# A graph layer and a mixture of experts on one core: the products' first two units taken by half and by quarters of Y, with the last rows and x blocks among them

## What is computed

```python
def gnn(H, W, A):                       # H = layernorm(x): (8, 2048, 128)
    HW = einsum('bnf,fo->bno', H, W)
    A_norm = relu((A + A.T) * 0.5)      # A = adj: (2048, 2048)
    D = sum(A_norm, axis=1)
    d_inv_sqrt = where(D > 0, D ** -0.5, 0)
    L_norm = eye(N) - d_inv_sqrt[:, None] * A_norm * d_inv_sqrt[None, :]
    return relu(einsum('nm,bmo->bno', L_norm, HW))

x = x + gnn(layernorm(x), W, adj)
tokens = layernorm(x)
# top 2 of 8 experts by softmax(tokens @ router_w.T), weights normalised to sum 1
# moe = tokens + sum over experts e of c_e * (gelu(tokens @ w1[e] + b1[e]) @ w2[e] + b2[e])
out = x + moe
```

## Time and profile before

| what | us |
|---|---|
| median of three runs (lowest, highest) | 878.23 (877.77, 879.5) |
| the profiled execution, own time | 877.46 |
| its span, first to last instruction | 875.7 |
| TensorE busy | 839.2 (96%) |
| VectorE busy | 639.1 (73%) |
| ScalarE busy | 476.0 (54%) |
| GpSimd busy | 324.7 (37%) |

### The profile page before, as it was taken

How to read it: one execution, slowest core, us unless ns; L and a number is a source line. 1 busy time by engine, 2 the same in 40 slices (tenths; PEclk the granted TensorE clock), 3 DMA queues, 4 the chain that set the end, 5 groups by cost and what they waited for, 6 DMA issues and landing times.

```text
span 875.7 us, 14324 instructions
## 1 busy us (share of the span) xinstructions
PE 839.2 (96%) x4098; PEld 697.3 (80%) x4098; DVE 639.1 (73%) x1553; ACT 476.0 (54%) x871; POOL 324.7 (37%) x318
## 2 busy tenths in 40 slices
PE   3687999999999999999999999999999999999998
PEld 3676788888888888888888777788888888888886
DVE  3678645479889644443515599999999999999997
ACT  2686523224333201021110488888888888888886
POOL 1893163474757545555445539101000000000000
PEclk9999999999999999999999999999999999999999
DMA  9991576686866257977778876778767777778772
GB/s 277 325 311 53 220 284 253 240 277 237 272 221 202 85 181 285 334 273 263 255 280 315 303 249 230 267 281 294 289 272 265 257 274 277 273 290 292 286 266 82
DMA packets 93472, 223.00 MB, mean 255 GB/s; under 512 B 8904, under 2 KB 60128, under 8 KB 81520
## 3 DMA queue, kind: packets, MB, share of 16 engines
q1 hardware_dynamic: 88304, 213.23, 68.7%
q0 software_dynamic: 2608, 8.33, 2.4%
q10 hardware_dynamic: 2512, 0.86, 0.4%
HBM read 157.89 MB, written 64.49 MB: 254 GB/s over the span
## 4 chain that ended last, share of the span: by engine, by line
PE 90%; DVE 4%; ACT 2%; DMA 2%; issue 1%; DVEq 0%; ACTq 0%; SPq 0%
PE bank L989 13%; PE bank L991 13%; PE bank L990 13%; PE bank L1489 6%; PE bank L1473 6%; PE bank L1475 6%; PE bank L1486 6%; PE bank L1474 6%; PE bank L1487 6%; PE bank L344 3%; PE bank L936 2%; PE bank L1495 2%; PE bank L474 1%; PE bank L325 1%; DMA b_sb<-in_L_ffn_b 1%
## 5 line engine op out<-in xcount | busy, mean ns | idle before, releaser
L1531 ACT ACTIVATE act_h<-bank,b_sb 128x512 f32<-128x512 f32 x256 | 176.3, 689 | 46.8 <-PE bank L1475 42.5
L1573 DVE TENSOR_TENSOR gated<-c_all,act_h 128x512 f32<-128x512 f32 x256 | 177.4, 693 | 25.5 <-ACT act_h L1531 20.4
L1578 DVE TENSOR_TENSOR g_lo<-gated,g_hi 128x512 fp32r<-128x512 f32 x256 | 175.1, 684 | 0.2
L1538 ACT ACTIVATE g_hi<-gated 128x512 fp32r<-128x512 f32 x256 | 159.5, 623 | 6.1 <-DVE gated L1573 6.1
L1449 POOL DMA_DIRECT2D out<-fin x31 | 23.6, 762 | 308.6 <-DVE fin L1586 308.6
L1105 POOL TENSOR_SCALAR z<-x,mv,rstd 128x128 f32<-128x128 f32 x128 | 106.9, 848 | 3.4
L989 PE MATMUL bank<-y_hi,stage 128*128 128x512 f32 x256 | 105.4, 412 | 2.8 <-issue 1.6
L1051 ACT ACTIVATE z_hl<-bank 128x512 fp32r<-128x512 f32 x32 | 19.1, 597 | 156.4 <-PE bank L936 156.4
L1473 PE MATMUL bank<-z_e,w_hi 128*128 128x512 f32 x256 | 102.8, 402 | 0.1
L1489 PE MATMUL bank<-g_lo,w_hi 128*128 128x512 f32 x256 | 100.9, 394 | 1.1 <-DVE g_lo L1578 1.1
L989 PE MATMUL bank<-y,stage 128*128 128x512 f32 x256 | 101.2, 395 | 0.0
(11 more groups left out here) (133 smaller groups left out, 1487.4 us busy)
## 6 DMA issues: line engine op xcount, KB each, us to landing
c_all<-c_scratch SPq DMA_DIRECT2D x64, 1024.0 KB, 8.1
s_scratch<-stage SPq DMA_DIRECT2D x14, 2048.0 KB, 8.2
stage<-s_scratch SPq DMA_DIRECT2D x14, 2048.0 KB, 8.0
z_e<-z_scratch SPq DMA_DIRECT2D x32, 512.0 KB, 7.3
z_scratch<-z_hl SPq DMA_DIRECT2D x31, 512.0 KB, 2.7
x_raw<-in_x SPq DMA_DIRECT2D x32, 256.0 KB, 6.7
x_res<-in_x SPq DMA_DIRECT2D x32, 256.0 KB, 7.0
r_e<-res_scratch SPq DMA_DIRECT2D x32, 256.0 KB, 2.7
```

Source lines behind the costliest of these rows:

```text
L1531: act.activation(v.act_h[e % R][:, :], ps_h[e % 2][:, :], ACT.Gelu, bias=v.b1_sb[:, e:e + 1]).then_inc(gelu_done, 1)
L1538: act.activation(v.g_hi[e % R][:, :], v.gated[e % R][:, :], ACT.Copy).then_inc(hi_done, 1)
L1573: dve.tensor_tensor(out=v.gated[e % R][:, :], in0=v.c_all[s][:, e, :], in1=v.act_h[e % R][:, :], op=ALU.mult).then_inc(gated_done, 1)
L1578: dve.tensor_tensor(out=v.g_lo[e % R][:, :], in0=v.gated[e % R][:, :], in1=v.g_hi[e % R][:, :].bitcast(FP32), op=ALU.subtract).then_inc(lo ...
```

## The change

Unit 0 and unit 1 are taken in six parts: blocks 15 to 8 of unit 0, then of unit 1; 7 to 4 of each; 3 to 0 of each. The adding loop over rows ends with row 11 (`ROWS_APART`); the last four rows, ten blocks, are transposed behind the first products. x blocks 12 to 15 are loaded behind all rows (14 and 15 into two new buffers in Y's own place), and turned and projected among products (`after_first`). GpSimd's column adds end with row 6 (`LAST` = 9); those of j = 8 and 7 go to VectorE too. Column sums stand in three clusters. Group 0 of unit 0's stage is turned behind row 8, group 1 behind row 9.

```diff
-    ps_x, ps_p = v.banks[4], [v.banks[5] if k % 2 or k >= v.MB else v.banks[3] for k in range(v.U)]
+    BANK = [3 if k in range(0, 12, 2) else 6 if k in (12, 14) else 5 for k in range(v.U)]
+    ps_x, ps_p = v.banks[4], [v.banks[b] for b in BANK]
...
-        free = k - 3 if k < MB else k - 1
+        if k in (14, 15):
+            sp.wait_ge(v.summed, v.until_tenth)
...
@@ -334,10 +347,8 @@
         pe.wait_ge(xt_copied, k + 1)
         if k == 0:
             pe.wait_ge(w_centred, 1)
-        elif k < MB:
-            wait(pe, hw_kept, k - 1)
-        elif k == MB:
-            pe.wait_ge(hw_kept, k)
+        elif k <= MB:
+            wait(pe, hw_kept, last_before(BANK, k))
...
-    FIRST = [(0, None), (0, 0), (0, 1), (1, None), (1, 0), (1, 1), (0, 2), (0, 3), (1, 2), (1, 3)]
+    FIRST = [(0, 0), (0, 1), (0, None), (1, None), (1, 0), (1, 1), (0, 2), (1, 2), (0, 3), (1, 3)]
...
-    LAST = 6
-    PARTS_AT = {14: ((0, 1),), 8: ((1, None), (1, 0), (1, 1)), 7: ((0, 2),), 5: ((0, 3),), 3: ((1, 2),), 1: ((1, 3),)}
-    RELU_AT = {13: 2, 12: 1, 11: 0}
-    ADD_AT = {13: 4, 11: 3, 10: 2, 9: 1}
-    JOBS = [2, 2, 2, 2, 1, 1, 1, 1, 1, 1, 1, 1, 0, 0, 0, 0]
+    LAST = 9
+    ROWS_APART = 12
+    JOBS = [2, 2, 2, 2, 1, 1, 1, 1, 0, 0, 0, 0, 0, 0, 0, 0]
+    EARLY = sum(JOBS)
...
+        for k in range(EARLY, MB):
+            pr.load(sp, k)
...
```

GpSimd, ScalarE, TensorE in `setup_stage`:

```diff
-            if r == 10:
+            if r == 9:
                 root(0)
+        pr.invert(pool, [EARLY])
         root(1)
+        for k in range(EARLY + 1, MB):
+            pr.invert(pool, [k])
...
+            for k in [k - 1 for k in jobs(r) if k]:
+                pr.keep(act, k)
+            if r == 8:
+                pr.keep(act, EARLY - 1)
+            if r in (8, 9):
+                st.high_group(act, 0, r - 8)
+            if r == 10:
+                st.high_direct(act, 0)
+                for m in range(15, 11, -1):
+                    y_high(m)
+        for m in range(11, 7, -1):
             y_high(m)
-            if m in RELU_AT:
-                relu(MB - 1 - RELU_AT[m], RELU_AT[m], 0)
-            if m == 7:
-                pr.keep(act, MB - 1)
-            for u, g in PARTS_AT.get(m, ()):
-                if g is None:
-                    st.high_direct(act, u)
-                else:
-                    st.high_group(act, u, g)
+        st.high_direct(act, 1)
+        st.high_group(act, 1, 0)
+        st.high_group(act, 1, 1)
+        for r in range(ROWS_APART, MB):
+            relu(r, MB - 1 - r, 0)
+        pr.copy_x(act, 12)
+        act.wait_ge(pr.xt_turned, EARLY)
+        act.wait_ge(pr.x_mv_done, EARLY)
+        st.high_group(act, 0, 2)
+        y_high(7)
+        y_high(6)
+        pr.keep(act, 12)
+        pr.copy_x(act, 13)
+        st.high_group(act, 1, 2)
+        y_high(5)
+        y_high(4)
+        pr.keep(act, 13)
+        pr.copy_x(act, 14)
+        st.high_group(act, 0, 3)
+        y_high(3)
+        pr.keep(act, 14)
+        pr.copy_x(act, 15)
+        st.high_group(act, 1, 3)
+        y_high(2)
+        pr.keep(act, 15)
+        y_high(1)
+        y_high(0)
...
         pe.wait_ge(small_in, 16 * v.small_loads)
         pr.average_w(pe)
-        for r, j in enumerate(ROWS):
+        for r, j in enumerate(ROWS[:ROWS_APART]):
...
+            if r == 6:
+                for k in (15, 14, 13, 12):
+                    column_sum(k)
+            if r == 8:
+                pr.project(pe, 11)
+                st.turn_group(pe, 0, 0)
+            if r == 9:
+                for k in (11, 10, 9, 8):
+                    column_sum(k)
+                pe.wait_ge(pr.hw_kept, EARLY - 1)
+                st.turn_group(pe, 0, 1)
+        v.column_sum, v.turn_last = column_sum, turn
```

VectorE in `setup_stage`, and TensorE in `graph_stage`:

```diff
+                st.low_group(dve, 0, 0)
+            if r == 10:
+                st.low_group(dve, 0, 1)
+                add_columns(8)
+                st.low_direct(dve, 0)
+                y_low(15)
+                y_low(14)
             if r == 11:
-                add_columns(5)
-        st.low_direct(dve, 0)
-        st.low_group(dve, 0, 0)
-        for m in range(MB - 1, -1, -1):
-            y_low(m)
-            if m in ADD_AT:
-                add_columns(ADD_AT[m])
-            for u, g in PARTS_AT.get(m, ()):
-                if g is None:
-                    st.low_direct(dve, u)
-                else:
-                    st.low_group(dve, u, g)
-                if (u, g) == (1, 0):
-                    degrees(1)
-            if m == 3:
-                outward()
+                add_columns(7)
+        y_low(13)
+        add(12, 3, 0)
+        y_low(12)
+        add(13, 2, 0)
+        y_low(11)
+        add(14, 1, 0)
+        y_low(10)
+        add(15, 0, 0)
+        y_low(9)
+        y_low(8)
+        st.low_direct(dve, 1)
+        st.low_group(dve, 1, 0)
+        st.low_group(dve, 1, 1)
+        for j in range(6, 0, -1):
+            add_columns(j)
+        pr.statistics(dve, 12)
+        degrees(1)
+        st.low_group(dve, 0, 2)
+        y_low(7)
+        y_low(6)
+        pr.statistics(dve, 13)
+        st.low_group(dve, 1, 2)
+        y_low(5)
+        y_low(4)
+        pr.statistics(dve, 14)
+        st.low_group(dve, 0, 3)
+        y_low(3)
+        pr.statistics(dve, 15)
+        st.low_group(dve, 1, 3)
+        y_low(2)
+        y_low(1)
+        outward()
+        y_low(0)
...
+            if u == 2 and i == 1:
+                st.turn_group(pe, 2, 2)
+                st.turn_group(pe, 2, 3)
+            if i == (5 if u == 2 else 2):
...
+        def after_first(u, m):
+            if u == 0 and m >= 8:
+                if m in (14, 13, 12, 11):
+                    v.turn_last(26 - m, m - 11, 0)
+                if m == 11:
+                    st.turn_group(pe, 1, 0)
+                if m == 10:
+                    st.turn_group(pe, 1, 1)
+            elif m >= 8:
+                if m == 14:
+                    pr.turn_x(pe, 12)
+                if m == 12:
+                    st.turn_group(pe, 0, 2)
+                if m == 11:
+                    pr.project(pe, 12)
+                    pr.turn_x(pe, 13)
+                if m == 10:
+                    for k in range(7, -1, -1):
+                        v.column_sum(k)
+                if m == 9:
+                    st.turn_group(pe, 1, 2)
+            elif u == 0:
+                if m == 6:
+                    pr.project(pe, 13)
+                    pr.turn_x(pe, 14)
+                if m == 4:
+                    st.turn_group(pe, 0, 3)
+                if m == 2:
+                    pr.project(pe, 15)
+            else:
+                if m == 6:
+                    pr.project(pe, 14)
+                    pr.turn_x(pe, 15)
+                if m == 5:
+                    st.turn_group(pe, 1, 3)
+                if m == 3:
+                    st.turn_group(pe, 2, 0)
+                    st.turn_group(pe, 2, 1)
-        for part in range(4):
+        for part, (a, b) in enumerate([(15, 8), (15, 8), (7, 4), (7, 4), (3, 0), (3, 0)]):
+            for m in range(a, b - 1, -1):
+                after_first(u, m)
```

57 lines of the change are left out of this document (16 added, 41 removed).

## The result

Seven runs of the changed kernel took 885.04 us in the median (883.15 to 888.16), seven of the kernel before beside them 878.23 (875.28 to 880.44). The ratio is 1.0086, 95% interval 1.0067 to 1.0105: slower by 5.9 to 9.2 us. The forecast was 884.3, range 880.8 to 887.5.

What follows compares the result with a forecast made beforehand. TensorE was taken to bound the kernel, with everything to win or lose before about 108 us. -8.5 + 7.0 + (8.3 - 1.3) + 0.6 = +6.1 us gave a forecast of 884.3 us, range 880.8 to 887.5.

Steps and rivals of the forecast that it cites:

- Step 1: From row 9's arrival to the first product: it starts at 70.1 instead of 78.6 us, 8.5 us earlier.
- Step 2: Behind the first product: four x blocks, ten blocks of rows 12 to 15 and eight column sums, 7.0 us.
- Step 3: New TensorE waits between the start and unit 2: 8.3 us against 1.3 before.
- Step 4: TensorE's lower clock over the first two blocks and row 12: 0.6 us later, bounds none and 1.6.
- a root doesn't hold VectorE up: Rival: at the start the diagonals run beside GpSimd's root; 2.3 us less, 882.0 us; chance 7%.
- the next rival: Rows 8 and 9 land earlier, first product at 65.6 us, deciding sign 66.1 or earlier; 879.2 us, not slower; chance 8%.
- y(7): After unit 1's upper half TensorE waits for the lower half's column sums, degrees, root, high and low part: 2.2 us.
- y(1): Behind x 15's projection TensorE waits, as ScalarE keeps that projection before making y(1)'s high part: 2.7 us.
- y(2): TensorE waits for unit 1's last transposes, copied by ScalarE, then the high and low part: 0.75 us.
- (a): At the start TensorE waits for y(13), behind VectorE's adds of row 11 and a column add: 1.8 us.
- (c): TensorE waits for y(5), behind VectorE's statistics of x 13, a low group and GpSimd's root: 0.85 us.
- more time at the low clock: Rival: the clock also falls behind the waits for y(7) and y(1), 0.7 and 1.6 us; 885.9 to 886.6 us; 25%.

Runs made afterwards that it cites:

- e3: Changed kernel plus 20 unread transposes of the identity ahead of the first product; 884.93 us, ratio 1.0079 to the kernel before.
- e8: Changed kernel plus unread transposes filling three waits: 20 at the start, 20 ahead of y(7), 24 ahead of y(1); 883.59 us, ratio 1.0051.
- the five kernels named above the table: Changed kernel and those with column adds on GpSimd, x 12 and 13 loaded early, rows filled, or the last two together; to unit 2 within 0.7 us.
- e10: Kernel before plus unread transposes filling three waits in the stage of rows, ahead of projections 3, 5 and 7; 875.01 us, ratio 0.9961.
- e11: Changed kernel plus the same three fills in the stage of rows, ahead of projections 3, 5 and 7; 884.99 us, ratio 1.0089.
- e2: Changed kernel with the eight column sums moved one block earlier, ahead of x 12's projection and x 13's turn; 883.70 us, ratio 1.0059.
- e1: Changed kernel with x 15 projected five blocks earlier, behind unit 1's block 4; 881.08 us, ratio 1.0036.
- e9: Changed kernel with projection 15 and the column sums moved earlier, the start and three waits among rows filled with unread transposes; 875.96 us, ratio 0.9974.
- e5: Changed kernel with the column adds of blocks 8 and 7 given from VectorE to GpSimd; 886.89 us, ratio 1.0091.

## Why the forecast was right, and where it was right by luck

By the steps of the prediction, at the comparison point. Measured is what the traces of the changed kernel, e3 and e8 give; the 7.8 is what the other rows leave of the 17.4 us by which the stretch behind the first product grew. The figures hold for the profiled execution, and the clock's is the one that differs most between executions (3.1 to 3.9 us between e8 and the five kernels named above the table).

| term | forecast | measured |
|---|---|---|
| 1, the start | -8.5 | -11.2 |
| 2, moved work | +7.0 | +7.8 |
| 3, new waits, less 1.3 before | +7.0 | +5.9 |
| 4, the clock | +0.6 | +3.7 |
| sum | +6.1 | +6.2 |

**Step 1 was 2.7 us too small.** 1.1 are row 9 (59.98 instead of 61.1). The two loads are worth 2.0 by e10 and e11, not 1.5; the rest is within the scatter of its arrival. 1.5 are the root: from row 9 to the first product I had 9.0 us, and 7.46 passed, since the diagonals don't wait. That was the rival *a root doesn't hold VectorE up*, which I gave 7%. The failed sentence is "I let them wait likewise and end 0.45 after the root": a row for a column add was carried over to a root. The diagonals ended 3.37 us behind row 9 and not 4.75, and the root bounded nothing. I had looked for the condition of the next rival, a first product by 66.1; it was not met. Of the named signs, the first product between 68 and 72 and the diagonals that end behind the root didn't appear; both long waits (2.11 at 90.30, 2.62 at 107.00) and unit 2 at 113.38 did.

**Step 2** left out that each of nine pieces put between blocks costs the interrupted block 0.09 us, though the price stood there (0.69 and 0.78): 0.8 in all. Turning an x block, on the other hand, costs 0.36 among products (79.44 to 79.80) and not 0.46, 0.4 less in all. The remaining 0.4 of the difference isn't assigned to anything.

**Step 3** held for the two waits that matter: y(7) 2.11 (forecast 2.2), y(1) 2.62 (2.7), y(2) 0.69 (0.75). The releaser named is the one that the trace shows for y(1) and y(2). e2 shows that the wait for y(7) is made by the order and goes with it; e1 shows it for 2.1 of the 3.3 us of the other two. (a) is 1.16 with the clock held up (1.00 and 0.16 in e8) instead of 1.8, (c) 0.35 in e8 instead of 0.85, the latter in line with a root that doesn't hold VectorE (held until 93.38, y(5)'s low part would have begun 0.6 later than at 92.80); at half speed (c) is hidden entirely. With them e8's waits sum to 1.16 + 2.2 + 0.35 + 0.69 + 2.8 = 7.2, less 1.3. That the column adds of 6 to 1 cost nothing held (they ended at 82.6, the sums came at 84.42), and no wait of TensorE up to unit 2 is left over for the store or the late loads of x.

**Step 4 failed.** "So I expect the lower level over the first two blocks" and its 0.6: the clock fell there for 6.6 us, which cost 1.3, and it fell behind both other long waits, at which the sum had it at nothing, for another 2.4. This is the rival *more time at the low clock*, which had 25%; it is what happened, with prices near those that it named (1.6 in full behind y(1), 0.7 behind y(7)). With the start as I had it and the other three terms as measured, the time would have been 887.1 (878.2 + 8.9); with the real start and a clock at full, 880.7. Two errors of 2.7 and 3.1 us, of opposite sign, and two smaller ones (0.8 and 1.1) that nearly cancel too, made the number: that it lies within 1 us of the measured one is luck.

**The direction** did not hang on luck. The head start is paid back in full by moved work and waits (11.2 against 7.8 + 5.9), and e9 against e10 shows it with the three falls among the rows out of both and no fall left in the new order: it ties at best.

## To carry to other kernels

Work that fills an engine's idle time ahead of its start doesn't vanish when the start moves ahead of it: count it behind the start, with the price of every interruption, before counting the head start as won. When a step is moved, look at what stands in the queue of the engine that makes the *next* input (ScalarE's keep ahead of y(1)'s high part), since a wait made by two orders cost 2.6 us here, and most of it went by moving one line. And price a wait of some 2 us of TensorE with the half-speed stretch behind it; in these kernels that was another 1.2 to 1.3 us where the clock fell, which isn't in each execution, and 20 to 24 idle transposes took it back.

## What was not expected of the hardware

- GpSimd's roots over eight and four columns (1.64 and 1.01 us) don't hold VectorE operations with two SBUF inputs (0.61 for two diagonals in the traces of all twelve kernels in the new order, 1.40 for two low parts); its column adds do (0.87 instead of 0.28, 3.24 instead of 1.41), and an operation with one PSUM input kept its 0.68 us beside an add. Why a root is different was not tested.
- Behind idle times of 2.1 to 2.6 us TensorE's granted clock fell to 0.5 in some executions and not in others, at a place where the kernels are alike (behind y(7)'s wait of 2.11 us: 0.50 in the changed kernel, 1.00 over 90 to 108 us in e5). With three such waits filled, ahead of any change, the kernel before took 3.6 us less. Of its scatter between runs it took only a part (5.0 to 3.6 us).
